# A new order of items on every engine in the recurrent stage of an eight-core kernel

## The reference

```python
x = x + attn_a(layernorm(x), ...)   # causal attention, 16 heads, windows of 1024
x = x + ffn(layernorm(x), ...)      # routing to 64 slots, slot attention, back to tokens
x = x + attn_b(layernorm(x), ...)   # the recurrent stage, below
x = x + ffn(layernorm(x), ...)

# attn_b, C = 1024 channels, 16 heads of N = 64
xx = shift(x) - x
lora = tanh((x + xx * maa_x) @ maa_w1)               # 5 parts of 32
xw, xk, xv, xr, xg = (x + xx * (maa_i + lora_i @ maa_w2_i) for each i)
r, k, v = xr @ Wr, xk @ Wk, xv @ Wv
g = tanh(xg @ gate_w1) @ gate_w2
w = exp(-exp(time_decay + tanh(xw @ decay_w1) @ decay_w2))
for each token t:  y_t = r_t (S + u k_t v_t);  S = w_t S + k_t v_t     # per head, S is 64 x 64
out = (groupnorm(y) * ln_g + ln_b) * g @ Wo
```

## Time and profile before

| | us |
|---|---|
| median of 3 runs | 2281.48 |
| lowest, highest | 2276.55, 2341.12 |
| the profiled execution | 2276.45 |
| its span, slowest core (core 4) | 2274.9 |
| shortest span of its 8 cores | 2259.1 |
| recurrent stage on core 4 | about 870 to 2010 |

### The profile page before, as it was taken

One profiled execution on the slowest core, in us unless ns is written; L12 is line 12 of the kernel. 1 busy time (PEld: TensorE's weight loads), 2 busy tenths in 40 slices (PEclk: granted clock), 3 DMA queues, 4 the chain that ended last, 5 costly groups with the idle time before them and its releaser, 6 DMA issues.

```text
span 2274.9 us, 43100 instructions; the slowest of 8 cores (2259.1 to 2274.9 us)
## 1 busy us (share of the span) xinstructions
PE 1765.3 (78%) x14642; PEld 994.0 (44%) x14810; DVE 1378.2 (61%) x2321; ACT 1080.7 (48%) x1707; POOL 849.8 (37%) x699
## 2 busy tenths in 40 slices
...
GB/s 180 104 31 69 103 87 105 102 104 118 106 165 205 216 175 159 102 38 57 48 74 75 65 48 66 75 75 50 72 75 66 47 66 66 75 175 219 155 269 336
DMA packets 92583, 251.65 MB, mean 111 GB/s; under 512 B 13232, under 2 KB 21425, under 8 KB 92372
## 3 DMA queue, kind: packets, MB, share of 16 engines
...
...
## 4 chain that ended last, share of the span: by engine, by line
PE 53%; DVE 12%; issue 11%; POOL 9%; ACT 9%; DMA 4%; DVEq 0%; ACTq 0%; SPq 0%; POOLq 0%
PE bF L1931 11%; PE aF L456 6%; PE aF L497 5%; PE f_F L1021 4%; PE bF L1941 3%; ACT Wslot L554 3%; PE aO L512 3%; PE aS L531 3%; PE bF L2045 3%; POOL xout L1832 2%; POOL xout L1836 2%; POOL htok L2507 2%; DVE b_m L2308 1%; PE f_C L1042 1%; PE aF L464 1%
## 5 line engine op out<-in xcount | busy, mean ns | idle before, releaser
L554 ACT ACTIVATE Wslot<-aS,cvals_s 128x1024 bf16<-128x1024 f32 (+3 forms) x384 | 327.5, 900 | 175.0 <-PE aS L531 173.9
L1931 PE MATMUL bF<-xout,Wslot 128*128 128x256 bf16 x2048 | 270.3, 292 | 21.9 <-ACT hfeat L2166 8.3
L1832 POOL TENSOR_TENSOR xout<-b_m,b_hf 128x1024 bf16<-128x1024 bf16 x128 | 250.3, 1967 | 64.7 <-DVE b_m L2308 64.6
L1931 PEld LDWEIGHTS bF<-xout,Wslot 128*128 128x128 bf16 x2048 | 205.1, 104 | 84.4 <-issue 47.5
L732 POOL TENSOR_SCALAR ave<-amv 128x1 f32<-128x1 f32 x36 | 9.2, 257 | 481.9 <-DVE amv L570 481.9
L2308 DVE TENSOR_TENSOR b_m<-bB,b_xx 128x1024 bf16<-128x1024 f32 x128 | 155.6, 1216 | 52.5 <-PE bB L1893 50.5
L531 PE MATMUL aS<-aQf,aKf 64*128 64x512 bf16 (+3 forms) x768 | 132.3, 340 | 25.3 <-ACT Wslot L554 18.8
L512 PE MATMUL aO<-aVaug,Wslot 128*128 128x65 bf16 x2304 | 129.2, 198 | 25.7 <-DVE Wslot L636 25.3
L2166 ACT ACTIVATE hfeat<-bF 128x512 bf16<-128x512 f32 x128 | 76.2, 595 | 150.5 <-PE bF L1931 150.4
L2496 POOL TENSOR_TENSOR b_rk<-hfeat 128x1024 bf16<-128x1024 bf16 x32 | 69.9, 2185 | 191.3 <-ACT hfeat L2166 191.3
L2045 PE MATMUL bF<-Wslot,b_ygT 128*128 128x512 bf16 x466 | 119.3, 393 | 15.0 <-issue 7.1
...
## 6 DMA issues: line engine op xcount, KB each, us to landing
xin<-x1d SPq DMA_DIRECT2D x64, 512.0 KB, 5.4
xin<-x3d SPq DMA_DIRECT2D x36, 512.0 KB, 9.5
xin<-x SPq DMA_DIRECT2D x32, 512.0 KB, 4.2
xout<-x SPq DMA_DIRECT2D x32, 512.0 KB, 5.2
x1d<-xout SPq DMA_DIRECT2D x32, 512.0 KB, 3.2
x2d<-xin SPq DMA_DIRECT2D x32, 512.0 KB, 2.7
xin<-x2d SPq DMA_DIRECT2D x32, 512.0 KB, 3.7
x3d<-xin SPq DMA_DIRECT2D x32, 512.0 KB, 5.4
```

Source lines behind the costliest of these rows:

```text
L554: e_ex.inc(a.activation(Pk[:, :, qo:512], psS[i % 2][:, :, 0:512 - qo], AF.Exp, bias=cvals[:, 1:2], scale=0.125), s)
L1832: return eng.tensor_tensor(dst, mm[:].rearrange("p (a o q) -> p a o q", a=2, o=2), hf[n % 2][:, 2 * s:2 * s + 2, :].unsqueeze(1).broadcast_to(
L1931: mm = t.matmul(ps[:, o * 256:(o + 1) * 256], w[:, dc, oc * 128:(oc + 1) * 128], mixb[:, sl, dc, :], start=(dc == 0), stop=(dc == NDC - 1))
```

## The change

All five lists in `around` (PE, ACT, DVE, POOL, SP) are replaced. No item is added to or taken from the work, and no instruction, wait or buffer of an item changes; but which item stands two before another in PSUM's turns follows from the new order. The new lists, in full; the lines that they replace are those of the listing above.

```diff
--- before.py
+++ after.py
@@ -1597,68 +1597,69 @@
             c = 2 * n
             return {
                 "pe": [
...
+                    ("E", c), ("WO", c - 2, 0), ("P2", c + 5, 1), ("V", n, 1, 1),
+                    ("Y", c), ("GW", n), ("LA", n + 1), ("WO", c - 2, 1),
+                    ("W", c + 1, 0), ("MX", n + 1, 0, 0), ("KT", c + 1), ("LB", n + 1),
+                    ("W", c + 1, 1), ("D", c + 1), ("YT", c - 1), ("MX", n + 1, 0, 1),
+                    ("MX", n + 1, 0, 2), ("WO", c - 1, 0), ("G", c, 0),
+                    ("MX", n + 1, 0, 3), ("Y", c + 1), ("G", c, 1), ("WO", c - 1, 1),
+                    ("YT", c), ("MX", n + 1, 1, 0), ("MX", n + 1, 1, 1), ("E", c + 1),
+                    ("K", n + 1, 0), ("DW", n + 1), ("K", n + 1, 1), ("PW", n + 1, 0),
+                    ("K", n + 1, 2), ("MX", n + 1, 1, 2), ("PW", n + 1, 1),
+                    ("LT", c + 4), ("MX", n + 1, 1, 3), ("G", c + 1, 0),
+                    ("PW", n + 1, 2), ("MX", n + 1, 2, 0), ("K", n + 1, 3),
+                    ("MX", n + 1, 2, 1), ("P2", c + 6, 0), ("G", c + 1, 1),
+                    ("PW", n + 1, 3), ("R", n + 1, 0), ("R", n + 1, 1),
+                    ("P2", c + 6, 1), ("R", n + 1, 2), ("V", n + 1, 0, 0),
+                    ("R", n + 1, 3), ("LT", c + 5), ("V", n + 1, 0, 1),
+                    ("V", n + 1, 1, 0), ("W", c + 2, 0), ("W", c + 2, 1), ("KT", c + 2),
+                    ("D", c + 2), ("P2", c + 7, 0),
                 ],
                 "act": [
...
+                    ("EX", c + 1, 2), ("XA", n + 1), ("EX", c + 1, 3), ("V", n, 1, 1),
+                    ("W", c + 1, 0), ("MX", n, 1, 0), ("SQ", c), ("GW", n),
+                    ("LA", n + 1), ("RB", c + 1), ("KT", c + 1), ("SB", c + 1),
+                    ("LB", n + 1), ("YT", c - 1), ("SQ", c + 1), ("MX", n, 1, 1),
+                    ("YT", c), ("K", n + 1, 0), ("MX", n, 1, 2), ("MX", n, 1, 3),
+                    ("W", c + 1, 1), ("LN", c + 4), ("SB", c + 2), ("MX", n, 2, 0),
+                    ("DW", n + 1), ("K", n + 1, 1), ("W", c + 2, 0), ("MX", n, 2, 1),
+                    ("PW", n + 1, 0), ("K", n + 1, 2), ("PW", n + 1, 1), ("LT", c + 4),
+                    ("PW", n + 1, 2), ("K", n + 1, 3), ("PW", n + 1, 3),
+                    ("MX", n + 1, 0, 0), ("W", c + 2, 1), ("LN", c + 5),
                     ("R", n + 1, 0), ("EX", c + 2, 0), ("R", n + 1, 1),
...
+                    ("EX", c + 2, 1), ("EX", c + 2, 2), ("R", n + 1, 2),
+                    ("EX", c + 2, 3), ("MX", n + 1, 0, 1), ("V", n + 1, 0, 0),
+                    ("R", n + 1, 3), ("LT", c + 5), ("MX", n + 1, 0, 2),
+                    ("V", n + 1, 0, 1), ("RB", c + 2), ("EX", c + 3, 0),
+                    ("V", n + 1, 1, 0), ("KT", c + 2), ("MX", n + 1, 0, 3),
+                    ("EX", c + 3, 1),
                 ],
                 "dve": [
...
+                    ("WO", c - 2, 0), ("P2", c + 5, 1), ("LS", c + 5), ("XXX", n + 1),
+                    ("MU", c + 1), ("RD", c), ("WO", c - 2, 1), ("W", c + 1, 0),
+                    ("MX", n + 1, 0, 0), ("W", c + 1, 1), ("D", c + 1),
+                    ("MX", n + 1, 0, 1), ("YN", c), ("MX", n + 1, 0, 2),
+                    ("WO", c - 1, 0), ("G", c, 0), ("G", c, 1), ("MX", n + 1, 0, 3),
+                    ("WO", c - 1, 1), ("RD", c + 1), ("SU", c + 1), ("MX", n + 1, 1, 0),
+                    ("MX", n + 1, 1, 1), ("YN", c + 1), ("PW", n + 1, 0),
+                    ("MX", n + 1, 1, 2), ("PW", n + 1, 1), ("G", c + 1, 0),
+                    ("MX", n + 1, 1, 3), ("PW", n + 1, 2), ("P2", c + 6, 0),
+                    ("G", c + 1, 1), ("PW", n + 1, 3), ("MX", n + 1, 2, 0),
+                    ("MX", n + 1, 2, 1), ("P2", c + 6, 1), ("MU", c + 2), ("LS", c + 6),
+                    ("W", c + 2, 0), ("D", c + 2), ("P2", c + 7, 0), ("SU", c + 2),
+                    ("W", c + 2, 1),
                 ],
                 "pool": [
...
+                    ("SA", c), ("XX", n + 1), ("LR", c + 4), ("DV", c), ("RK", c + 1),
+                    ("LR", c + 5), ("RS", c), ("MX", n + 1, 0, 0), ("DV", c + 1),
+                    ("MX", n + 1, 0, 1), ("MX", n + 1, 0, 2), ("MX", n + 1, 0, 3),
+                    ("SA", c + 1), ("RS", c + 1), ("MX", n + 1, 1, 0),
+                    ("MX", n + 1, 1, 1), ("MX", n + 1, 1, 2), ("MX", n + 1, 1, 3),
+                    ("AL", n + 1), ("MX", n + 1, 2, 0), ("MX", n + 1, 2, 1),
+                    ("RK", c + 2),
                 ],
                 "sp": [
...
+                    ("LN", c + 3), ("ST", c - 2), ("LN", c + 4), ("S2", c + 5),
                     ("S2", c + 6), ("ST", c - 1),
                 ],
             }[eng]
```

More of the change, by code:

```diff
@@ L1599, in around @@
                 "pe": [
-                    ("WO", c - 2, 0), ("W", c, 1), ("WO", c - 2, 1), ("Y", c), ("E", c),
-                    ("WO", c - 1, 0), ("LA", n + 1), ("GW", n), ("MX", n + 1, 0, 0),
-                    ("MX", n + 1, 0, 1), ("D", c + 1), ("KT", c + 1), ("LB", n + 1),
-                    ("W", c + 1, 0), ("G", c, 0), ("G", c, 1), ("W", c + 1, 1),
-                    ("MX", n + 1, 0, 2), ("Y", c + 1), ("MX", n + 1, 0, 3),
-                    ("E", c + 1), ("WO", c - 1, 1), ("MX", n + 1, 1, 0),
@@ L1617, in around @@
+                    ("D", c + 2), ("P2", c + 7, 0),
                 ],
                 "act": [
-                    ("MX", n, 1, 3), ("XA", n + 1), ("EX", c + 1, 1), ("MX", n, 2, 0),
-                    ("EX", c + 1, 2), ("SQ", c), ("EX", c + 1, 3), ("SB", c + 1),
-                    ("RB", c + 1), ("LA", n + 1), ("LN", c + 4), ("GW", n),
-                    ("KT", c + 1), ("LB", n + 1), ("MX", n, 2, 1), ("SQ", c + 1),
-                    ("MX", n + 1, 0, 0), ("DW", n + 1), ("MX", n + 1, 0, 1),
@@ L1636, in around @@
+                    ("V", n + 1, 1, 0), ("KT", c + 2), ("MX", n + 1, 0, 3),
+                    ("EX", c + 3, 1),
                 ],
                 "dve": [
-                    ("WO", c - 2, 1), ("XXX", n + 1), ("SU", c), ("RD", c),
-                    ("WO", c - 1, 0), ("MU", c + 1), ("MX", n + 1, 0, 0), ("D", c + 1),
-                    ("MX", n + 1, 0, 1), ("YN", c), ("W", c + 1, 0), ("W", c + 1, 1),
-                    ("MX", n + 1, 0, 2), ("G", c, 0), ("G", c, 1), ("MX", n + 1, 0, 3),
@@ L1649, in around @@
-                    ("W", c + 2, 0), ("W", c + 2, 1), ("WO", c, 0),
+                    ("WO", c - 2, 0), ("P2", c + 5, 1), ("LS", c + 5), ("XXX", n + 1),
[4 more added lines that the diff above has]
+                    ("WO", c - 1, 1), ("RD", c + 1), ("SU", c + 1), ("MX", n + 1, 1, 0),
@@ L1658, in around @@
-                    ("DV", c + 2), ("RK", c + 3),
+                    ("SA", c), ("XX", n + 1), ("LR", c + 4), ("DV", c), ("RK", c + 1),
[4 more added lines that the diff above has]
+                    ("AL", n + 1), ("MX", n + 1, 2, 0), ("MX", n + 1, 2, 1),
@@ L1659, in around @@
+                    ("RK", c + 2),
                 ],
                 "sp": [
-                    ("S2", c + 5), ("LN", c + 4), ("ST", c - 2), ("LN", c + 5),
+                    ("LN", c + 3), ("ST", c - 2), ("LN", c + 4), ("S2", c + 5),
                     ("S2", c + 6), ("ST", c - 1),
```

35 lines of the change are left out of this document (removed).

## The result

The new order took 2285.89 us (median of six runs, 2281.78 to 2326.69), the old one beside it 2276.15 (median of six). The ratio is 1.004, with an interval of 1.0025 to 1.0054: no difference at 2%, but a small one in the wrong direction, 10 us longer where 33 us less was forecast. 2285.9 lies inside the range of 2200 to 2290, near its high end, in rival 2's stretch. (The cores of one die are at times disturbed by a lower clock; such executions are left out of every ratio here, and of kernel e5_mx2_early only one of six executions then remains.)

A forecast was written before the change was run, and what follows sets the result against it. PE bounds the kernel, with POOL setting the time for 25 us per block. New block 51.8 + 8.8 + 2.0 = 62.6 us, 2.2 under 64.8; 15 times that is 33, giving 2248 us; range 2200 to 2290, its own 2231 to 2266.

The forecast's parts named there:

- rival 2: PE's waits only change places: G's 1.1, five boundary waits, about three slow stretches; 64.5 to 65 us per block, 2281; chance 0.22.
- The old block: Steady block before the change: 64.8 us less 1.9 of slow-clock time on the path gives 62.9 at full clock.
- Changes of form: PE's switches between product shapes: 40 before, 39 after, 34 with a full side in both; worth 0 to 0.2 us, taken as 0.
- POOL's move: MX(n+1,2,*) behind AL leaves POOL's run from XX to DV; Y's 1.42 us wait for DV goes nearly whole.
- The 3.3 us of waits: PE's waits removed by moving MX on POOL and LN on ACT: at Y, MX, GW and KT, 3.3 us in all.
- The queues: SP's load for P2(c+7,0) lands with four us to spare; on DVE, SU ahead of W(c+2,1) costs nothing.
- The walk: PE's new list followed item by item through one block: 51.8 us of work plus 8.8 of waits, 60.6 at full clock.
- The clock: Slow stretches on PE after small items with waits: one and a half per block, 2.0 us; bounds none and four.
- three places of small items: In PE's new list: LT, G, PW behind K2; W, KT, D, P2, E; KT, LB, W, D, YT; slow stretches could follow.
- Fifteen times one block: Sixteen blocks have 15 intervals, so 2.2 us saved per block gives 33 us; ramp and run-out unchanged.
- Rival 3: Slower by the clock: PE at 1.2 GHz in four stretches of 1.7 us, 67.4 per block; 2320 to 2345; chance 0.09 with beyond.

The follow-up runs named there:

- e5_mx2_early: Old order with one POOL move, MX(n+1,2,0) and MX(n+1,2,1) behind AL(n+1), against the kernel before: 2258.12 us in its one value.
- e12: Old order with full-size idle products filling seven of PE's waits, POOL's list unchanged, against the kernel before: ratio 0.9901.
- e11: Old order with MX(n+1,2,*) behind AL on POOL and seven PE waits filled with idle products, against the kernel before: 2222.83 us, ratio 0.9771.

## Why the prediction was wrong, by its steps

- **The old block, 62.9 at full clock with 1.9 lost to slow stretches: right.** e12 has 62.94, and rounds 3 to 13 of before 64.85, so 1.9. The place was partly off: R0 alone loses 1.5 on the mean of the rounds, 1.3 in the block that I had read, and the last WO 0.5.
- **Changes of form, 0: right as far as seen.** The traces have 39 before and 38 after, 34 with a full side in both, and nothing in the runs needs a price for them.
- **POOL's move, no longer 25 us that set the time: right.** Y's wait is gone and MX stands behind AL as said. At full clock the old order with this move alone is 1.7 us per block faster (e12 against e11). The 3.3 us of waits that I had taken off contain LN's move on ACT as well, which was not tested alone.
- **The queues: right.** P2(c+7,0) waits for KT's take-out on ACT and not for its load, and Y for no W.
- **The walk, 60.6: 0.7 too low.** Its waits were 8.8 us in sum; those in the block shown are 9.4. G waited 1.16 (1.1), R2 0.52 (0.5), D 0.55 (0.6), V(1,1) 0.73 (0.6), P2(c+7,0) 0.38 (0.6), K0 0.70 (0.4), Y nothing (0.1). One wait was mis-sized: W 1.80 against 0.4. I had priced MU by its first product beside POOL's MX. Its middle product, a form of its own, took 3.15 beside RK and 1.21 alone. So the order gives 1.6 us at full clock, not 2.3.
- **The clock, 2.0 us per block: the step that failed.** It was 4.9 in rounds 3 to 13, with a granted clock of 0.90 where 0.92 to 0.97 was said. I had found three places of small items, and counted one and a half slow stretches at 1.3 us, on the ground that the waits were shorter in sum (8.8 against 9.9). In the block shown three items or pairs run at 0.50: K3 loses 2.92 - 1.91 = 1.0, R0 with R1 5.32 - 3.66 = 1.7, WO 3.05 - 1.89 = 1.2; 3.8 in all, where this block exceeds 61.31 by 3.7. K3 and R0 stand behind the first of my three places, WO behind the second; behind the third (KT, LB, W, D, YT) the clock held. On the mean of all rounds these items lose 4.4 of the 4.9. The sum of the waits was the wrong measure: it is hardly shorter than before (9.4 against 9.9), while the time at 1.2 GHz rose from 121 to 175 us. What in the new places brings the clock down oftener, the waits or the small items beside them, stays open, as does which of the four other lists does it.
- **Fifteen times one block: not quite.** The last two rounds gain 5.6 us, which hides more than a third of what the first thirteen lose.
- **Sum.** Forecast 60.6 + 2.0 = 62.6. Measured in rounds 3 to 13 61.3 + 4.9 = 66.2. Against before there: -1.6 + 3.0 = +1.3 per block. The first thirteen rounds make 14.8 us, the last two take 5.6 off, and 9.2 remain. That the time lies inside 2200 to 2290 is the width of the range; the direction was wrong.

Rival 2 (64.5 to 65 us per block, 2281) came nearest: its G 1.1, the waits around the boundary and "about three slow stretches". Rival 3's mechanism, the clock, is what did it, at less than its four full stretches (67.4). I gave them 0.22 and 0.09 and the forecast 0.45. The evidence stood in my own text: three places listed, PE on the path at nearly all. With three stretches counted at the 1.3 us of R0, the sum would have been 60.6 + 3.9 = 64.5, or 2277: still short, as R0's loss in one block (1.3) was below the mean (1.5).

The Trainium skill (TensorE: Matmul & The Clock Gate, "A second HAM failure mode: psum-queue depth-cycling") says that idling between groups of products while cycling PSUM banks makes the clock oscillate. The traces agree: in the block shown waits of 0.3 to 1.8 us, most of them for a PSUM turn, stand before each of the three stretches at 0.50, and products of full size put into these waits take the clock from 0.90 to 0.99.
